# The low-rank mixing of a recurrent layer: stacked rounded operands for full fp32 products, and a new order of the pieces

## The chip, the cores and the metric

One core of one Trainium2 chip runs the kernel as a single program. The metric is device time in microseconds.
## The reference

Two layers work on 16 sequences of 1024 tokens with 256 features. Each has an attention-like part and an experts part, and adds their gated product. The change touches the recurrent part of the first layer alone. Cut to what matters:

```
delta  = shifted - h                       # h: normalised input, shifted by a token
x_lerp = h + delta * x_proj_mu
x0 = tanh(x_lerp @ xl_w1.T) @ xl_w2.T + xl_b2          # rank 32, then 5*32
x1 = tanh(x0).reshape(B, T, 5, 32)
x2 = einsum('btnr,hnr->btnh', x1, x_out_w)             # five mixes of width 256
mus = x2 + x_bias
r = (h + delta*mus[0]) @ r_w.T;  w = tanh((h + delta*mus[1]) @ w_w1.T) @ w_w2.T + w_b
k, v, g likewise from mus[2], mus[3], mus[4]
wd = exp(-exp(w))
# per step t:  o_t = r_t S + (r_t * bonus * k_t) v_t ;  S = S * wd_t + k_t v_t
# then o is normalised per head, scaled, gated by silu(g), and multiplied by o_w
```

All of it is fp32, and the result has to keep about that accuracy.

## The kernel before

Four stages follow each other: routing with the layer norm (to 282 us), the recurrence (282 to 1880), the experts of layer 0 (to 3480), and layer 1. The recurrence works on 32 groups of 512 tokens (4 sequences by 128 tokens, `GN` columns), features on partitions. The groups run in passes of four (`Fori` over j, four values of q).

Inside a group the recurrence over 128 tokens is done by seven *levels*: at level lv pairs of blocks of 2^lv tokens are joined. For each level TensorE makes 16 small products of K2 and R2 (L1408), VectorE multiplies K, R and the decay by decays (L1131 to L1135) and, at levels 0 to 4, copies the new products under a mask into A2 (L1144); ScalarE does that copy at levels 5 and 6 (L1263). Level lv + 1 needs both.

The projections of the *next* group are cut into *pieces* (0 to 9), and the output work of the previous group into *chunks*. `sequence` (L847) writes out by hand for every engine in which of nine slots s each of them comes: level s, then chunk, then piece in most slots. In slots 0 and 1 the own group's last pieces stand (values and gates). The pieces:

- piece 0: LOW, two products of `w1` with lerp, tanh on ScalarE into `low` (32 rows);
- piece 1: X0 and X0T, `w2` by `low`, tanh into `x1` (128 rows, four of the mixes) and `x1t` (32 rows, the fifth). `low`, `w2`, `xo` and `xot` are padded with zeros to 128 rows;
- pieces 2, 3, 4, 6, 7: two of the ten mixing products each (`mixes`, L1336), `xo` by `x1`, indices `MIX`. VectorE makes tmp = (product + bias) * delta (L1105), GpSimd adds h into `mix` (L1018);
- piece 3 ends with DLOW (first decay product), piece 4 with DEXP and KEY, piece 5 is REC, piece 7 begins with OWN, piece 8 is VAL, piece 9 GATES.

All these products land in two PSUM banks in turn (`bank`, L844): a product with index n may start only when the one with index n - 2 has been read (`room`, `emptied`). A product of a mix needs both halves of that mix from GpSimd (`have_mix`). `begin` makes lerp of group f + 2 on VectorE at the end of slot 8 (L1089); `ahead` makes its delta on GpSimd behind slot 7 (L1004). VectorE also does one round of the router's top-k search in each group (slots 5, 6 and 7).

Of the kernel before, what the change touches and what calls it, by code (L numbers as in the profile page):

```python
# [676 lines left out]
def recurrence_phase(nc, ctx, ps, ps_heads, xnT_d, s0_d, acc_d, left_d, ident, score, idxT, gateT, idxL, gateL, w):  # L677

    with ExitStack() as mem:
# [10 lines left out]
        w1 = sb("a_w1", [P, KD, RANK])  # L690
        w2 = sb("a_w2", [P, NMU * RANK])
        b2 = sb("a_b2", [P, 1])
        b2t = sb("a_b2t", [RANK, 1])
        xo = sb("a_xo", [P, NMU - 1, D])
        xot = sb("a_xot", [P, D])
# [17 lines left out]
        low = sb("a_low", [P, GN])  # L713
        x1 = sb("a_x1", [P, GN])
        x1t = sb("a_x1t", [P, GN])
# [55 lines left out]
        th_sb = sem("a_th_sb")  # L771
        rkb = sem("a_rkb")
# [37 lines left out]
        LOADS = 21  # L810
        PADDED = 7
# [9 lines left out]
        USES = 22  # L821
        BY_ACT = [LOW, X0, X0T, DLOW, DEXP, KEY, REC, OWN, VAL, VAL + 1]
        BY_DVE = MIX + [GATES, GATES + 1]
        AT = {2: (0, 1), 3: (2, 3), 4: (4, 5), 6: (6, 7), 7: (8, 9)}
# [19 lines left out]
        def bank(n):  # L844
            return ps[6 + n % 2]

        def sequence(eng, ahead, begin, piece, level, chunk, extra=None):  # L847

            def group(j, q, first, left):
# [11 lines left out]
                def piece_at(s):  # L861
                    if s < LATE:
                        piece(g, q, FRONT + s, first)
                    elif left:
                        piece(g + 1, f1[1], s - LATE if s < CHUNK else s - LATE + 1, False)

                for s in range(SLOTS):
                    if s < LEVELS:
                        level(g, r, s, first)
                    if left and s == CHUNK:  # L870
                        piece(g + 1, f1[1], CHUNK - LATE, False)
                    if extra and s == CHUNK:
                        extra(g, s)
                    if s < LATE or s == SLOTS - 1:
                        piece_at(s)
                        chunk_at(s)
                    else:
                        chunk_at(s)
                        piece_at(s)
                        if extra and s < CHUNK:  # L880
                            extra(g, s)
# [7 lines left out]
            for s in range(FRONT):  # L889
                piece(0, 0, s, True)  # L890
# [15 lines left out]
        def _(sp):  # L906
            loads = [(mu[:], w["L0_attn_x_proj_mu"]), (w1[:], w["L0_attn_xl_w1"]),
                     (b2[:], w["L0_attn_xl_b2"][0:P]), (b2t[:], w["L0_attn_xl_b2"][P:P + RANK]),
                     (xb[:], w["L0_attn_x_bias"]),
# [4 lines left out]
            for dst, src in loads:  # L914
                sp.dma_start(dst, src).then_inc(w_in, 16)
            padded = [(w2[0:RANK, :], w["L0_attn_xl_w2"]), (dw2[0:GATE, :], w["L0_attn_w_w2"]),
                      (xot[0:RANK, :], w["L0_attn_x_out_w"][P:P + RANK])]
            padded += [(xo[RANK * n:RANK * (n + 1), n, :], w["L0_attn_x_out_w"][RANK * n:RANK * (n + 1)])
                       for n in range(NMU - 1)]
            sp.wait_ge(set_up, PADDED)  # L920
            for dst, src in padded:
                sp.dma_start(dst, src).then_inc(w_in, 16)
            assert len(loads) + len(padded) == LOADS + 1

# [49 lines left out]
        def _(pool):  # L974
            nc.gpsimd.memset(zeros[:], 0.0).then_inc(zeroed, 1)
            for operand in (xo, w2, xot, dw2, low, x1t, dlow):
                nc.gpsimd.memset(operand[:], 0.0).then_inc(set_up, 1)
# [15 lines left out]
            pool.wait_ge(w_in, 16 * (LOADS + 1))  # L993
# [44 lines left out]
        def _(dve):  # L1038
# [32 lines left out]
            dve.wait_ge(w_in, 16 * (LOADS + 1))  # L1071
# [19 lines left out]

            def piece(f, q, s, first):
                r = q % 2
                if s == 5:
# [19 lines left out]
            def level(g, r, lv, first):  # L1114
# [5 lines left out]
                if lv == LATE:  # L1120
                    gates(g, r)
# [74 lines left out]
        def _(act):  # L1196
# [9 lines left out]
            def piece(f, q, s, first):  # L1206
                r = q % 2

                def ready(n):
                    act.wait_ge(piece_ps, USES * f + n + 1)  # L1210
                    return bank(n)
# [1017 lines left out]
```

## Time and profile before

| | us |
|---|---|
| median of 3 runs | 4614.92 |
| lowest, highest | 4613.5, 4615.97 |
| span of the profiled execution | 4612.0 |
| TensorE busy in it | 4189.6 |
| VectorE busy | 2751.5 |
| ScalarE busy | 1976.9 |
| GpSimd busy | 1694.4 |
| recurrence (one group x 32) | 282 to 1880 |

Times in rows are microseconds from the start of the profiled execution, and a duration of a row that merges several instructions reaches from the first one's start to the last one's end. Matmuls overlap: the next one starts before the end that the profile gives to the one before. A product in fp32 shows as two matmul records, one in the rounded type fp32r as one. What stands in brackets is the idle time of the engine before the row, and who ended it.

### The profile page before, as it was taken

How to read it: one execution, taken by the hardware profiler on the slowest of the kernel's cores; microseconds unless marked ns; L12 is line 12 of the kernel's file. 1: busy time of each engine (PE TensorE's matmuls, PEld its weight loads, DVE VectorE, ACT ScalarE, POOL GpSimd, SP SyncE). 2: the span in 40 equal slices, each digit the busy share in tenths (PEclk: the TensorE clock that was granted, in tenths of full speed). 3: DMA queues.
4: the chain of work that ended last, by engine and by line, in shares of the span. 5: the costliest groups of instructions: out<-in, count | busy, mean ns of one | idle time of the engine just before them, and what ended most of it. 6: DMA issues, size and time to landing. Idle time of an engine off the chain costs nothing. (4 is left out here: it accounts for less than half of the span.)

```text
span 4612.0 us, 79916 instructions
## 1 busy us (share of the span) xinstructions
PE 4189.6 (91%) x28828; PEld 3314.9 (72%) x28828; DVE 2751.5 (60%) x5151; ACT 1976.9 (43%) x3701; POOL 1694.4 (37%) x1338
## 2 busy tenths in 40 slices
PE   6759999999999999799999999999995989999985
PEld 6636555555555556698888989898995878777774
DVE  4447777777767777334343433434433688888886
ACT  2214444444444444444454444445442444444441
POOL 1123333333333333344444444444432233333333
PEclk9999999999999999899999999999997999999998
DMA  6611011011011010223223232323224334444433
GB/s 205 214 44 38 29 38 34 29 38 34 29 38 34 29 38 29 81 42 64 48 56 60 41 66 43 62 47 59 42 40 92 93 98 111 105 95 111 101 61 41
DMA packets 254043, 294.80 MB, mean 64 GB/s; under 512 B 21600, under 2 KB 226656, under 8 KB 251616
## 3 DMA queue, kind: packets, MB, share of 16 engines
q0 software_dynamic: 88064, 117.74, 15.2%
q1 hardware_dynamic: 140000, 138.26, 9.3%
q10 hardware_dynamic: 25600, 33.56, 2.2%
q8 instruction: 260, 4.26, 0.4%
q14 instruction: 119, 0.97, 0.1%
HBM read 155.15 MB, written 134.35 MB: 63 GB/s over the span
## 5 line engine op out<-in xcount | busy, mean ns | idle before, releaser
L523 DVE TENSOR_TENSOR e_hTl<-e_hf,e_hTh 128x512 fp32r<-128x512 f32 x512 | 355.0, 693 | 795.4 <-ACT e_hTh L465 795.4
L1018 POOL TENSOR_TENSOR a_mix<-a_tmp,a_h 128x512 f32<-128x512 f32 x320 | 393.9, 1251 | 808.4 <-DVE a_tmp L1105 651.9
L384 POOL DMA_INDIRECT acc_d<-e_y,e_sids x256 | 402.0, 1570 | 715.6 <-DVE e_y L539 670.8
L464 ACT ACTIVATE e_hf<-ps_heads,e_b 128x512 f32<-128x512 f32 x512 | 355.3, 694 | 697.8 <-PE ps_heads L611 690.6
L611 PE MATMUL ps<-e_w2h,e_hTh 128*128 128x256 f32 x2048 | 580.1, 283 | 0.0
L611 PE MATMUL ps<-e_w2h,e_hTl 128*128 128x256 f32 x2048 | 576.5, 281 | 0.0
L611 PE MATMUL ps<-e_w2l,e_hTh 128*128 128x256 f32 x2048 | 571.3, 279 | 0.0
L611 PE MATMUL ps_heads<-e_xTh,e_w1h 128*128 128x512 f32 x1024 | 419.4, 410 | 26.8 <-issue 22.8
L611 PE MATMUL ps_heads<-e_xTh,e_w1l 128*128 128x512 f32 x1024 | 407.6, 398 | 0.0
L611 PE MATMUL ps_heads<-e_xTl,e_w1h 128*128 128x512 f32 x1024 | 407.2, 398 | 0.4 <-issue 0.3
L611 PEld LDWEIGHTS ps<-e_w2h,e_hTh 128*128 128x128 f32 x2048 | 385.0, 188 | 19.8
L611 PEld LDWEIGHTS ps<-e_w2h,e_hTl 128*128 128x128 f32 x2048 | 385.0, 188 | 17.8
L611 PEld LDWEIGHTS ps<-e_w2l,e_hTh 128*128 128x128 f32 x2048 | 386.7, 189 | 0.0
L1408 PEld LDWEIGHTS ps_heads<-a_R,a_K 32*128 32x128 f32 x7168 | 227.0, 188 | 205.9 <-issue 204.2
L465 ACT ACTIVATE e_hTh<-ps_heads,e_b 128x512 fp32r<-128x512 f32 x512 | 351.3, 686 | 0.0
L1105 DVE SCALAR_TENSOR_TENSOR a_tmp<-ps,a_xb,a_delta 128x512 f32<-128x512 f32 x320 | 239.3, 750 | 174.9 <-PE ps L1317 160.8
L361 POOL DMA_INDIRECT e_x<-xn_d,e_gids x256 | 269.8, 1054 | 190.2 <-PE ps_heads L595 112.4
L1408 PE MATMUL ps_heads<-a_R,a_K 32*128 32x64 f32 x7168 | 256.8, 278 | 62.9 <-DVE a_A L1144 34.2
L1144 DVE COPY_PREDICATED a_A<-a_mask,ps_heads 128x1024 f32<-128x1024 uint32 x160 | 274.4, 1715 | 0.0
L1317 PE MATMUL ps<-a_x,a_xo 128*128 128x512 f32 x512 | 246.6, 604 | 0.7 <-ACT a_R L1231 0.7
L611 PEld LDWEIGHTS ps_heads<-e_xTh,e_w1h 128*128 128x128 f32 x1024 | 195.8, 191 | 66.9 <-issue 28.5
L611 PEld LDWEIGHTS ps_heads<-e_xTl,e_w1h 128*128 128x128 f32 x1024 | 195.3, 191 | 47.4
(294 smaller groups left out, 9458.6 us busy)
## 6 DMA issues: line engine op xcount, KB each, us to landing
r_x<-in_L_attn_hidden_states SPq DMA_DIRECT2D x32, 512.0 KB, 4.6
xn_d<-r_xn ACTq DMA_DIRECT2D x32, 512.0 KB, 3.1
xnT_d<-r_xT ACTq DMA_DIRECT2D x32, 512.0 KB, 3.6
acc_d<-a_zeros POOLq DMA_DIRECT2D x32, 512.0 KB, 3.0
s_d<-a_s SPq DMA_DIRECT2D x32, 512.0 KB, 2.8
e_w<-in_L_ffn_w SPq DMA_DIRECT2D x16, 1024.0 KB, 4.8
f_a<-acc_d SPq DMA_DIRECT2D x32, 512.0 KB, 3.8
f_x<-s_d SPq DMA_DIRECT2D x32, 512.0 KB, 5.2
```

Of the source, the lines that this page charges most:

```text
L361: pool.indirect_dma_start(xg[r][:, t, :], None, xn_d, bass.IndirectOffsetOnAxis(ap=gids[:, GT * q + t:GT * q + t + 1], axis=0)).then_inc(x ...
L384: pool.indirect_dma_start(acc_d, bass.IndirectOffsetOnAxis(ap=sids[:, GT * q + t:GT * q + t + 1], axis=0), ys[r][:, t, :], None, compute_o ...
L464: nc.scalar.activation(hf[m % 2][:], ps[2 + m % 2][:], ACT.Gelu, bias=b1s[:, m:m + 1])
L465: nc.scalar.activation(hT[q % 2][0][:, m, :], ps[2 + m % 2][:], ACT.Gelu, bias=b1s[:, m:m + 1]).then_inc(hi_sb, 1)
L523: nc.vector.tensor_tensor(hT[q % 2][1][:, m, :], hf[m % 2][:], hT[q % 2][0][:, m, :].bitcast(F32), ALU.subtract).then_inc(h_sb, 1)
L611: last = nc.tensor.matmul(out, lhsT, rhs, start=(first and n == 0), stop=(end and n == len(pairs) - 1))
L1018: nc.gpsimd.tensor_tensor(mix[n][:, m, :].rearrange("p (c t) -> p c t", c=GT), tmp[i % 2][:].rearrange("p (c t) -> p c t", c=GT), h[q % 2] ...
L1105: stt(out=tmp[i % 2][:], in0=bank(MIX[i])[:], scalar=xb[:, n, m:m + 1], in1=delta[r][:, m].rearrange("p c t -> p (c t)"), op0=ALU.add, op1 ...
L1144: nc.vector.copy_predicated(a4, m4.unsqueeze(1).to_broadcast([P, NH * GT, nb, half]), pairs_ps(half)).then_inc(A_sb, 1)
L1317: done = nc.tensor.matmul(to, lhsT, rhs, start=(k == 0), stop=(k == len(pairs) - 1))
L1408: done = nc.tensor.matmul(ps_heads[:, hd, c * P:c * P + P // 2].rearrange("p (n t) -> p n t", t=half), K2[r][rows, tok], R2[r][rows, tok]. ...
```

## The change

`low` and the five `x1` tiles become rounded (fp32r) operands of 128 rows: four blocks of 32 rows that hold, from the top, high, high, low, low parts of the same 32 values (the high part is the value rounded, the low part what the rounding left). The weights `w2` and `xo` hold high, low, high, low in the same rows. One rounded pass over 128 rows so adds up all four partial products, where a full fp32 product over 32 meaningful rows stood. To this end

- the host lays `w1`, `w2`, `b2` and `x_out_w` out fourfold, and `xl_w2`'s product is made once for each of the five mixes (X[0] to X[4]) instead of X0 and X0T;
- ScalarE makes the tanh into `whole[k % 2]`, 128 rows, and a rounding copy into the operand (`stack`); VectorE subtracts on rows 64 to 127 (`remainder`). That is done six times in each group (LOW and five X);
- before the first group ScalarE rounds `w2` and `xo`, and VectorE subtracts on two blocks of 32 rows of each (four instructions); GpSimd's fills with zeros shrink from seven to two, the 22 loads of weights become 17;
- there are 13 pieces, and `sequence` places them by tables, some of them between the level and the chunk of a slot, or ahead of the level. DEXP now comes ahead of level 6, the mixing products stand around DLOW, KEY and OWN instead of in pairs, and X[4] with REC comes ahead of the chunk in slot 7;
- 25 bank uses in a group instead of 22; being odd, they make the bank depend on q too.

```diff
-        LATE = 2
-        FRONT = SLOTS - LATE + 1
-        MIX = [3, 4, 5, 6, 8, 9, 13, 14, 16, 17]
-        LOW, X0, X0T, DLOW, DEXP, KEY, REC, OWN, VAL, GATES = 0, 1, 2, 7, 10, 11, 12, 15, 18, 20
-        AT = {2: (0, 1), 3: (2, 3), 4: (4, 5), 6: (6, 7), 7: (8, 9)}
+        PIECES = 13
+        AHEAD_OF_LEVEL = {6: 6, 7: 8}
+        AHEAD_OF_CHUNK = {0: 11, 1: 12, 4: 2, 5: 4, 8: 10}
+        BEHIND_CHUNK = {2: 0, 3: 1, 4: 3, 5: 5, 6: 7, 7: 9}
+        OWN_PIECES = (11, 12)
+        MIX = [4, 5, 7, 9, 11, 13, 16, 17, 18, 20]
+        X = [1, 2, 3, 6, 14]
+        LOW, DLOW, DEXP, KEY, REC, OWN, VAL, GATES = 0, 8, 10, 12, 15, 19, 21, 23
+        AT = {3: (0, 1), 5: (2, 3), 7: (4, 5), 9: (6, 7), 10: (8, 9)}
+        X_AT = {1: (0, 1), 2: (2,), 4: (3,), 8: (4,)}
...
                 for s in range(SLOTS):
+                    piece_at(AHEAD_OF_LEVEL.get(s))
                     if s < LEVELS:
                         level(g, r, s, first)
-                    if left and s == CHUNK:
-                        piece(g + 1, f1[1], CHUNK - LATE, False)
                     if extra and s == CHUNK:
                         extra(g, s)
+                    piece_at(AHEAD_OF_CHUNK.get(s))
+                    chunk_at(s)
+                    piece_at(BEHIND_CHUNK.get(s))
...
(VectorE)
+            for part, raw in ((xo, xor), (w2, w2r)):
+                for top in (RANK, 3 * RANK):
+                    nc.vector.tensor_tensor(part[top:top + RANK], raw[top:top + RANK],
+                                            part[top:top + RANK].bitcast(F32), ALU.subtract).then_inc(w_split, 1)
...
+            def remainder(f, k, part):
+                dve.wait_ge(high_sb, STACKS * f + k + 1)
+                nc.vector.tensor_tensor(part[P // 2:P, :], whole[k % 2][P // 2:P, :], part[P // 2:P, :].bitcast(F32),
+                                        ALU.subtract).then_inc(stacked, 1)
...
+                if s == 0:
+                    remainder(f, 0, low)
+                for k in X_AT.get(s, ()):
+                    remainder(f, 1 + k, x1[k])
...
(ScalarE)
+                def stack(k, n, part, **bias):
+                    to = ready(n)
+                    if not first or k >= 2:
+                        act.wait_ge(stacked, STACKS * f + k - 1)
+                    nc.scalar.activation(whole[k % 2][:], to[:], ACT.Tanh, **bias).then_inc(act_out, 1)
+                    emptied(act, f, n)
+                    nc.scalar.copy(part[:], whole[k % 2][:]).then_inc(high_sb, 1)
...
(TensorE)
+                    pe.wait_ge(stacked, STACKS * f + 2 + k)
+                    product(to[:], [(xo[:, order[k], m * P:(m + 1) * P], x1[k][:])]).then_inc(piece_ps, 1)
...
+                if s == 5:
+                    mixes(2)
+                    have_mix(0)
+                    whole_product(DLOW, GATE, [(dw1[:, k, :], mix[1][:, k, :]) for k in range(KD)])
+                    mixes(3)
+                if s == 6:
+                    emptied(pe, f, DLOW)
+                    whole_product(DEXP, P, [(dw2[:], dlow[:])])
+                if s == 7:
+                    mixes(4)
+                    have_mix(1)
+                    whole_product(KEY, P, [(kw[:, k, :], mix[2][:, k, :]) for k in range(KD)])
+                    mixes(5)
+                if s == 8:
                     have_mix(2)
+                    whole_product(REC, P, [(rw[:, k, :], mix[0][:, k, :]) for k in range(KD)])
+                if s == 10:
+                    mixes(8)
                     to = room(OWN)
...
+                    mixes(9)
```

## Rows read from the trace of the kernel before

**Rows 1.** Busy time by stretches; columns: us, busy us of each engine (instructions), clock, DMA.
```profile
800.00:1200.00 400.00, 379.37 (x3229) 235.46 (x3228) 293.22 (x445) 175.49 (x381) 141.66 (x105) 0.98 0.10 35
```

**Rows 2.** Timeline, GpSimd: start us, us, engine, line, operation, operands, count [idle before].
```profile
841.42 1.88 POOL L1004 TENSOR_TENSOR a_delta<-a_h 128x1024 f32<-128x1024 f32 x1
...
867.57 2.50 POOL L1018 TENSOR_TENSOR a_mix<-a_tmp,a_h 128x512 f32<-128x512 f32 x2 [13.24 <-DVE a_tmp L1105]
...
887.00 2.30 POOL L1018 TENSOR_TENSOR a_mix<-a_tmp,a_h 128x512 f32<-128x512 f32 x2 [6.57 <-DVE a_tmp L1105]
...
889.28 1.88 POOL L1004 TENSOR_TENSOR a_delta<-a_h 128x1024 f32<-128x1024 f32 x1
...
891.13 2.95 POOL L1018 TENSOR_TENSOR a_mix<-a_tmp,a_h 128x512 f32<-128x512 f32 x2
```

**Rows 3.** Timeline, TensorE, one group and the start of the next loop pass.
```profile
841.91 0.65 PE L1434 MATMUL ps<-a_V,a_KT 128*32 128x64 f32 x32
...
845.29 1.12 PE L1408 MATMUL ps_heads<-a_R,a_K 32*128 32x64 f32 x32
...
846.34 3.72 PE L1317 MATMUL ps<-a_vw,a_mix 128*128 128x256 f32 x16
...
856.60 1.90 PE L1317 MATMUL ps<-a_lerp,a_w 128*32 128x512 f32 x4
...
859.13 1.12 PE L1408 MATMUL ps_heads<-a_R,a_K 32*128 32x64 f32 x32 [0.62 <-DVE a_A L1144]
...
865.48 1.88 PE L1317 MATMUL ps<-a_x,a_xo 128*128 128x512 f32 x4
...
872.13 1.93 PE L1317 MATMUL ps<-a_mix,a_dw 128*64 128x512 f32 x4
...
880.13 1.88 PE L1317 MATMUL ps<-a_mix,a_rw 128*128 128x512 f32 x4
...
884.88 1.94 PE L1317 MATMUL ps<-a_x,a_xo 128*128 128x512 f32 x4
...
886.96 1.05 PE L1364 MATMUL ps<-a_heads,a_rk 128*128 128x4 f32 x8
...
895.68 0.87 PE L1408 MATMUL ps_heads<-a_R,a_K 32*128 32x64 f32 x19 [2.47 <-issue]
...
899.55 1.12 PE L1408 MATMUL ps_heads<-a_R,a_K 32*128 32x64 f32 x13 [3.00 <-issue]
...
900.60 5.21 PE L1317 MATMUL ps<-a_vw,a_mix 128*128 128x256 f32 x16
```

**Rows 4.** Timeline, VectorE, the same group.
```profile
861.09 1.24 DVE L1144 COPY_PREDICATED a_A<-a_mask,ps_heads 128x1024 f32<-128x1024 uint32 x1
...
868.96 1.40 DVE L1133 TENSOR_TENSOR a_R<-a_R,a_decays 128x256 f32<-128x256 f32 x1
...
886.08 1.52 DVE L1105 SCALAR_TENSOR_TENSOR a_tmp<-ps,a_xb,a_delta 128x512 f32<-128x512 f32 x2 [1.93 <-PE ps L1317]
...
891.89 2.74 DVE L1089 SCALAR_TENSOR_TENSOR a_lerp<-a_delta,a_mu,a_h 128x512 f32<-128x512 f32 x2
```

**Rows 5.** Timeline, TensorE, rounded products in the last stage.
```profile
3603.01 0.39 PE L2058 MATMUL ps_heads<-f_xTh,f_w1h 128*128 128x512 f32 x1
3603.24 0.39 PE L2058 MATMUL ps_heads<-f_xTh,f_w1l 128*128 128x512 f32 x1
```

**Rows 6.** Timeline, ScalarE, the same group.
```profile
861.79 0.69 ACT L1216 ACTIVATE a_x<-ps,a_b 128x512 f32<-128x512 f32 x1
```

**Rows 7.** Groups by line, experts stage; busy us, mean ns of one, idle before.
```profile
L441 ACT CAST e_w2h<-e_w 128x512 fp32r<-128x512 f32 x32 | 21.0, 656 | 0.0
...
L523 DVE TENSOR_TENSOR e_hTl<-e_hf,e_hTh 128x512 fp32r<-128x512 f32 x512 | 355.0, 693 | 795.4 <-ACT e_hTh L465 795.4
```

**Rows 8.** Timeline, TensorE, transposes behind two waits in the last stage.
```profile
3669.96 1.09 PE L2051 MATMUL ps_heads<-ident,f_xn 128*128 128x128 f32 x8 [2.81 <-ACT f_xn L1958]
...
3702.20 1.65 PE L2051 MATMUL ps_heads<-ident,f_xn 128*128 128x128 f32 x8 [2.85 <-ACT f_xn L1958]
```

More of the change, by code:

```diff
@@ L712, in recurrence_phase @@
         lerp = sb("a_lerp", [P, KD, GN])
-        low = sb("a_low", [P, GN])
-        x1 = sb("a_x1", [P, GN])
-        x1t = sb("a_x1t", [P, GN])
+        whole = [sb(f"a_whole{r}", [P, GN]) for r in range(2)]
+        low = sb("a_low", [P, GN], F32R)
+        x1 = [sb(f"a_x{k}", [P, GN], F32R) for k in range(NMU)]
         tmp = [sb(f"a_tmp{r}", [P, GN]) for r in range(2)]
@@ L809, in recurrence_phase @@
         NMM = NMU * KD
-        LOADS = 21
-        PADDED = 7
+        LOADS = 17
+        PADDED = 2
         SET = PADDED + 8
@@ L888, in sequence @@
             begin(0, 0, True)
-            for s in range(FRONT):
-                piece(0, 0, s, True)
+            for s in range(PIECES):
+                if s not in OWN_PIECES:
+                    piece(0, 0, s, True)
             ahead(1, 0, 1)
@@ L975, in _ @@
             nc.gpsimd.memset(zeros[:], 0.0).then_inc(zeroed, 1)
-            for operand in (xo, w2, xot, dw2, low, x1t, dlow):
+            for operand in (dw2, dlow):
                 nc.gpsimd.memset(operand[:], 0.0).then_inc(set_up, 1)
@@ L1346, in piece, with whole_product @@
+                    product(to[:], [(xo[:, order[k], m * P:(m + 1) * P], x1[k][:])]).then_inc(piece_ps, 1)
+                def whole_product(n, rows, pairs):
+                    product(room(n)[0:rows, :], pairs).then_inc(piece_ps, 1)
                 if s == 0:
                     pe.wait_ge(lerped, 2 * f + 2)
-                    product(room(LOW)[0:RANK, :], [(w1[:, k, :], lerp[:, k, :]) for k in range(KD)]).then_inc(piece_ps, 1)
-                if s == 1:
-                    to = room(X0)
-                    emptied(pe, f, LOW)
-                    product(to[:], [(w2[:, 0:P], low[:])]).then_inc(piece_ps, 1)
-                    to = room(X0T)
-                    pe.sem_inc(spare, 1)
-                    product(to[0:RANK, :], [(w2[:, P:P + RANK], low[:])]).then_inc(piece_ps, 1)
@@ L1356, in piece @@
-                if s == 5:
-                    to = room(REC)
+                    whole_product(LOW, P, [(w1[:, k, :], lerp[:, k, :]) for k in range(KD)])
+                for k in X_AT.get(s, ()):
+                    pe.wait_ge(stacked, STACKS * f + 1)
+                    whole_product(X[k], P, [(w2[:, order[k], :], low[:])])
+                if s in (3, 9):
+                    for i in AT[s]:
+                        mixes(i)
+                if s == 5:
+                    mixes(2)
+                    have_mix(0)
+                    whole_product(DLOW, GATE, [(dw1[:, k, :], mix[1][:, k, :]) for k in range(KD)])
+                    mixes(3)
@@ L1366, in piece @@
                     done.then_inc(piece_ps, 1)
-                for i in AT.get(s, ()):
-                    mixes(i)
-                if s == 3:
-                    to = room(DLOW)
-                    have_mix(0)
-                    product(to[0:GATE, :], [(dw1[:, k, :], mix[1][:, k, :]) for k in range(KD)]).then_inc(piece_ps, 1)
-                if s == 4:
-                    to = room(DEXP)
-                    emptied(pe, f, DLOW)
-                    product(to[:], [(dw2[:], dlow[:])]).then_inc(piece_ps, 1)
-                    to = room(KEY)
-                    have_mix(1)
-                    product(to[:], [(kw[:, k, :], mix[2][:, k, :]) for k in range(KD)]).then_inc(piece_ps, 1)
-                if s == 8:
+                    mixes(9)
+                if s == 11:
                     for u in range(2):
```

133 lines of the change are left out of this document (60 added, 73 removed).

## Prediction

> **What bounds the kernel now.** I read three views in this order. First the busy time by stretches: in the recurrence TensorE is busy 379.37 of 400 us, VectorE 293.22, ScalarE 175.49, GpSimd 141.66 [rows 1]. So TensorE is the obvious bound, and the change takes work from it. A share says nothing about what takes its place, so next come the timelines of one group (batch group of 512 tokens; 32 of them in four-group loop passes). GpSimd's delta starts at 841.42 and again at 889.28: a group takes 47.86 us [rows 2]. TensorE has a gap of 0.62 us before level 3, released by VectorE's level 2, and is otherwise all but full [rows 3]. Last, the starts of a loop pass: in every fourth group level 0 comes in two pieces after gaps of 2.47 and 3.00 us that nothing in the trace releases, and the value product behind it takes 5.21 us where 3.72 is usual [rows 3]; nothing in the change touches that, and I keep its price.
>
> Two limits thus alternate inside a group. From the lerps to level 3 VectorE leads: it works without a pause through levels 0 to 2 and what stands between them, and TensorE's level 3 at 859.13 waits for it [rows 3]. From 859.13 on TensorE leads, to the operand product of MIX 6 at 884.88, whose tmp VectorE starts at 886.08 [rows 3, 4]. Then GpSimd takes over: mix at 887.00, delta at 889.28, mix again at 891.13, and the two lerps end at 894.63 between them [rows 2, 4], which starts the next round.
>
> **What the change saves on TensorE.** An fp32 product of 512 columns is two records. Four of them started at 865.48, 0.43 apart (1.88 less the last record's 0.59, by three): a product occupies 0.85 us [rows 3]. A rounded (fp32r) product is one record, and in the last stage these start 0.23 apart (3603.01, 3603.24) and end 0.39 after their start [rows 5]. The ten mixing products go from 8.5 to 2.3 us, the two X products (1.7 us) become five of 0.23 (1.15). TensorE loses 6.2 + 0.55 = 6.8 us of a group, 218 us in 32.
>
> **What it adds.** Six times a group a tile now goes through tanh, a rounding copy on ScalarE and a subtraction on VectorE, where tanh alone stood (three times). The tanh takes 0.69 [rows 6]; the copy from SBUF to fp32r 0.656, the subtraction 0.693, both from the same forms in the experts stage [rows 7]. The subtraction works on 64 partitions here; the last stage's 64-row forms cost the same, so I take 0.69 (bounds: 0.62, since neighbours overlap, and 1.8, if it must let one GpSimd instruction of 1.15 end first). VectorE gains 3.9 us of a group, to about 39 of 47.9: no bound by its sum, but it works in order. ScalarE gains 5.8 and stays half idle. So a product's way to a usable operand becomes 0.39 + 0.69 + 0.66 + 0.69 + about 0.2 of handovers, 2.6 us, and these steps are placed in front of level work on VectorE.
>
> **The new path, step by step** (clock of the profile; level 3 still starts at 859.13, since all before it is VectorE's old work).
> 1. The low tile's subtraction comes before level 3 on VectorE. LOW ends at about 858.5 [rows 3], then 0.59 + 0.66 + 0.69: 860.5, 0.2 after VectorE was to start level 3. A level on VectorE is 0.78 of products (TensorE's level 3 ended at 860.25, handed over in 0.06, the copy began at 861.09) and the 1.24 of the predicated copy [rows 3, 4]: level 3 ends 862.5 (862.3 before).
> 2. X[0] and X[1] both stand between level 3 and level 4. ScalarE is free of the gate's activations at 861.79 [rows 6]. Tanh, copy, tanh, copy, each pair 1.3: 864.5; subtraction 865.2; level 4 on VectorE ends 867.1 (865.8 before). TensorE stands idle here; its saving of 2 us is gone.
> 3. Then subtraction, gate (the same shape) and the first tmp: 0.69 less the overlap of neighbours, twice, and half of tmp's 1.52 [rows 4, 7]: 869.1. GpSimd's two mixes need 0.17 + 1.15 + 1.15, and VectorE's K product of level 5 gets in between them with about 0.3 (three products take the 0.78 above): before, with the same three, R took 1.40 and ended at 870.36, after the second mix at 870.07 [rows 2, 4]. Both mixes are there, and DLOW starts, at 872.0. Before: 872.13 [rows 3]. All that TensorE saved up to here is gone.
> 4. DLOW 1.9, its tanh 0.6, DEXP 0.85, level 6 1.05, mix 4 0.23: KEY starts at 876.7, and mix 5 comes behind KEY's 1.71, at 878.4. Its result after 0.55, tmp 0.75, 0.17, GpSimd 1.15, 0.15: REC starts at 881.2. Before: 880.13 [rows 3]. Here TensorE waits some 2.5 us with only X[4] (0.23) in it.
> 5. REC to MIX 6 is unchanged, 4.75 us (884.88 less 880.13): 885.9. Result 0.55 later: tmp 6 starts 886.5 against 886.08 [rows 3, 4].
> 6. From tmp 6 on GpSimd's queue sets the pace, as before: first mix 0.92 later, delta 2.28 after that, and 5.35 on the lerps are done [rows 2, 4]. So the group gets 0.4 us longer, not 6.8 shorter.
>
> The sum: three of four groups +0.4. In the fourth the lerps are hidden by the loop's gap, and TensorE itself counts: MIX 8 waits for tmp 6 (887.4), OWN for tmp 7 (888.1), then 0.9 for OWN (a row of 1.05, less its last end), 0.23, and 3.4 from the state product (841.91) to level 0 (845.29) [rows 3]: level 0 at 892.6 against 845.29 + 47.86 = 893.15, -0.5. Eight passes: 8 x (3 x 0.4 - 0.5) = +5.6 us. Ahead of the first group VectorE gets four splits (widths 1280 and 640, twice; 0.69 per 512 elements gives 1.7 + 0.9 each, at most 5.2), minus the fills that GpSimd no longer makes (about 2) and a somewhat faster front (1 to 3): 0 to +3, say +1. The 1.1 MB more of weights lie beside VectorE's masks and first top-k round. Profiled time 4612 + 7 = 4619; the median stands 3 above the span: 4621, 0.15% above 4614.92. What a measurement can tell here is about 0.2%.
>
> VectorE and GpSimd alternating in step 3 is what the Trainium skill says in "SBUF — State Buffer", section "SBUF: two separate sides": an instruction of VectorE with both inputs in SBUF and one of GpSimd that reads SBUF take a shared port pair in turns, whole instruction by whole instruction. By that rule, the trace agrees: R took 1.40 and ended after the mix. The new subtractions are of this kind.
>
> **The rivals.** (a) The path is shorter than I made it. In step 6 VectorE now comes to the first lerp at about 891.3, when delta ends, 0.6 earlier than before (891.89). If the lerp goes ahead of the mix there, the lerps end 0.9 earlier than the old order gives. With step 5's +0.4 that is -0.5 in three groups, and -0.5 in the fourth as in my sum: 32 x -0.5 = -16, with the 1 us ahead and the median's 3 about 4600. For it: VectorE is no longer late. Against: delta and mix are neighbours in one queue (start to start 1.85), VectorE learns of delta by a semaphore. A handover less in steps 2 to 4 gives the same size; down to 4570.
> (b) TensorE's saving comes through for a good part, if VectorE's waits for X are not in the way of the levels. All of it is 4615 - 218 = 4397; a half, 4506. Against: steps 2 to 4 each rest on an order in the code.
> (c) Slower, by the clock. Where TensorE waits in step 4, it may come back at 1.2 GHz. In the last stage one wait of 2.81 us left the transposes behind it at 1.09 us, another of 2.85 us made them 1.65 [rows 8]; after the loop's gaps the value product took 5.21 for 3.72 [rows 3], +1.5. At +1.5 in each group: 4621 + 48 = 4669. It decides from the wait before REC: 2.5 us with 0.23 of work inside is just short of those two. The Trainium skill, "TensorE: Matmul & The Clock Gate", section "HAM oscillation — how this bites in real kernels", names gaps of idleness between bursts as what lowers the clock; by that rule this is the rival that the change invites.
> (d) Slower, by more collisions of the six subtractions with GpSimd's mixes: each costs up to 1.15. One more on the path in each group: 4621 + 37 = 4658, half of that 4640.
>
> **Chances.** My sum 0.35 (its own range 4605 to 4640: 0.25 within 0.2%, 0.03 faster, 0.07 slower); (a) 0.30 (0.27 faster, 0.03 same); (b) 0.07; (c) 0.10; (d) 0.18. Faster 0.37, same 0.28, slower 0.35. Both signs are about as likely, since the sum is a difference of two long chains in which each handover is known to 0.1 us and 32 groups multiply it. The range leaves out (b) and the ends of (a), (c): 4550 to 4665.
>
> **What would show it.** In the new profile: TensorE about 6 us idle in a group; it waits for VectorE before levels 4 and 5, and for GpSimd's mixes before DLOW and before REC (2 us or more there). VectorE waits for ScalarE at the subtraction of X[1]. From DVE tmp 6 to the lerps' end 8.5 us as now; delta to delta near 48.2. Wrong if delta to delta is under 47, if TensorE stays gapless, or if the granted clock falls in the middle of groups.

## The result and the profile after

| | us |
|---|---|
| median after (4 runs) | 4788.06 (4778.39 to 4794.64) |
| median before, same chip (4 runs) | 4615.44 (4613.5 to 4621.8) |
| ratio, 95% interval | 1.0372 (1.0357 to 1.0387) |
| span of the profiled execution after | 4793.0 |

The kernel got 3.7% slower, 173 us. I had forecast 4621 with a range to 4665; this lies outside it, beyond the price of rival (c). Each engine's line in the page, and the granted clock in 40 slices:

```profile
PE 4212.8 (88%) x28540; PEld 3433.2 (72%) x28540; DVE 2890.8 (60%) x5347; ACT 2159.2 (45%) x3991; POOL 1696.3 (35%) x1333
...
PEclk9988898888889888989999999999999899999998
```

The clock line of before:

```profile
PEclk9999999999999999899999999999997999999998
```

TensorE is busy 4212.8 us where it was 4189.6, although the change took some 218 us of products from it. The clock line says why: slices 3 to 18 hold the recurrence of after, and 13 of the 16 show an 8; in the line of before, slices 3 to 16 all show a 9, and only slice 17, in which its recurrence ends, an 8. The same stretch as [rows 1], with its columns:

```profile
800.00:1200.00 400.00, 350.02 (x2827) 243.25 (x2827) 291.39 (x439) 198.52 (x413) 131.52 (x96) 0.85 0.09 30
```

And the longer stretch by which kernels are compared below, TensorE alone (us, busy us and instructions, granted clock, DMA share, GB/s), after:

```profile
400.00:1600.00 1200.00, 1049.26 (x8549) 0.86 0.09 30
```

Before, the second one read:

```profile
400.00:1600.00 1200.00, 1143.60 (x9741) 0.99 0.10 34
```

TensorE went from 95% busy at 0.99 of full speed to 87% busy at 0.86. GpSimd's delta marks the groups. Two pairs of neighbours in the timeline of after:

```profile
369.32 1.89 POOL L1007 TENSOR_TENSOR a_delta<-a_h 128x1024 f32<-128x1024 f32 x1
417.60 1.89 POOL L1007 TENSOR_TENSOR a_delta<-a_h 128x1024 f32<-128x1024 f32 x1
...
913.47 1.88 POOL L1007 TENSOR_TENSOR a_delta<-a_h 128x1024 f32<-128x1024 f32 x1
968.09 1.89 POOL L1007 TENSOR_TENSOR a_delta<-a_h 128x1024 f32<-128x1024 f32 x1
```

One group takes 48.28 us, which is what I had forecast (48.2), another 54.62. Of the 31 distances one is 46.6, one 48.3, two are 49.8, two 51.5 to 51.7, all others 54 to 58. Before, they were 47.2 to 47.9 [rows 2], but for the first two (40.7 and 45.8) and five with the loop's gap in them, 55 to 56. The recurrence, which ended at 1880.0 before, ends at 2064.3, 184 us later; the stages behind it take 2728.7 us, where they took 2732.0.

**Where the 6.3 us of a group are.** The clock of the second group around REC and the state product, read in stretches:

```profile
903.00:907.00 4.00, 3.85 (x8) 0.58 0.34 135
907.00:913.00 6.00, 4.92 (x33) 1.00 0.00 0
913.00:925.00 12.00, 11.80 (x95) 0.57 0.16 45
925.00:947.00 22.00, 18.32 (x208) 1.00 0.01 2
```

There are two falls to 1.2 GHz (half of full speed) between this REC and the next, 2 x 0.42 x 4 = 3.4 us and 2 x 0.43 x 12 = 10.3 us long. TensorE's timeline at the same place:

```profile
901.33 0.49 PE L1346 MATMUL ps<-a_low,a_w 128*128 128x512 f32 x1 [0.45 <-ACT a_K L1254]
903.15 3.35 PE L1346 MATMUL ps<-a_mix,a_rw 128*128 128x512 f32 x4 [1.32 <-POOL a_mix L1021]
...
911.15 0.49 PE L1346 MATMUL ps<-a_x,a_xo 128*128 128x512 f32 x1 [0.77 <-DVE a_tmp L1122]
911.81 1.05 PE L1404 MATMUL ps<-a_heads,a_rk 128*128 128x4 f32 x8 [0.17 <-DVE a_tmp L1122]
...
913.64 0.93 PE L1460 MATMUL ps<-a_V,a_KT 128*32 128x64 f32 x32
...
921.73 4.88 PE L1346 MATMUL ps<-a_vw,a_mix 128*128 128x256 f32 x16
926.53 1.12 PE L1434 MATMUL ps_heads<-a_R,a_K 32*128 32x64 f32 x32
```

The group of 48.28 us:

```profile
369.55 0.65 PE L1460 MATMUL ps<-a_V,a_KT 128*32 128x64 f32 x32
...
378.17 1.12 PE L1434 MATMUL ps_heads<-a_R,a_K 32*128 32x64 f32 x32 [0.47 <-DVE a_A L1161]
...
392.33 3.23 PE L1346 MATMUL ps<-a_ow,a_og 128*128 128x256 f32 x8
...
409.13 1.98 PE L1346 MATMUL ps<-a_mix,a_rw 128*128 128x512 f32 x4 [1.09 <-POOL a_mix L1021]
...
417.83 0.65 PE L1460 MATMUL ps<-a_V,a_KT 128*32 128x64 f32 x32
```

From REC to the state product it is 10.49 us (913.64 less 903.15) against 8.70; from the state product to level 1, 12.89 (926.53 less 913.64) against 8.62. Together 6.1 of the 6.3 us. REC itself takes 3.35 for 1.98, and VAL 4.88 for the 3.72 of [rows 3]. The 48.28 us group has a fall too, at 392.33 (3.23 us where 1.89 is usual), but it takes the place of TensorE's waits before level 5 and X[3] and costs nothing: DLOW starts 9.15 us behind level 4 there and 9.31 in the second group, which has no fall at that place. So I read that a fall is paid only where the chain runs through TensorE.

### The profile page after: what moved, and what is told of

The parts are those of the page before. It is cut to its first block and busy times, and to the rows that moved or that the text cites. A ratio compares the mean times of both kernels' runs of the same rounds, so it can differ in the third digit from the quotient of the medians.

```text
span 4793.0 us, 80743 instructions
## 1 busy us (share of the span) xinstructions
PE 4212.8 (88%) x28540; PEld 3433.2 (72%) x28540; DVE 2890.8 (60%) x5347; ACT 2159.2 (45%) x3991; POOL 1696.3 (35%) x1333
## 5 line engine op out<-in xcount | busy, mean ns | idle before, releaser
L1434 PEld LDWEIGHTS ps_heads<-a_R,a_K 32*128 32x128 f32 x7168 | 251.4, 207 | 200.0 <-issue 196.3
L1434 PE MATMUL ps_heads<-a_R,a_K 32*128 32x64 f32 x7168 | 281.1, 298 | 85.4 <-DVE a_A L1161 84.1
L2025 ACT CAST f_hTh<-ps 128x512 fp32r<-128x512 f32 x160 | 93.9, 587 | 306.6 <-DVE ps L1845 306.6
L611 PEld LDWEIGHTS ps_heads<-e_xTl,e_w1h 128*128 128x128 f32 x1024 | 195.4, 191 | 47.5
```

The source lines that it names most:

```text
L611: last = nc.tensor.matmul(out, lhsT, rhs, start=(first and n == 0), stop=(end and n == len(pairs) - 1))
L1434: done = nc.tensor.matmul(ps_heads[:, hd, c * P:c * P + P // 2].rearrange("p (n t) -> p n t", t=half), K2[r][rows, tok], R2[r][rows, tok]. ...
L2025: nc.scalar.copy(hT[0][:, m, :], ps[4 + m % 2][:]).then_inc(hh_sb, 1)
```

## The experiments

My theory (A) after the result: the waits that the change opens in TensorE's queue lower its clock, twice in a group, and that is the whole loss but for a small rest. The rivals: (B) the longer chain of tanh, copy, subtraction, tmp and mix, or collisions on it, makes the groups longer, and the clock only follows; (C) the REC wait alone does it. "Filler" below is a rounded 256-column product whose result nobody reads, written to free columns of a PSUM bank; 6 of them take 0.87 us and 10 take 1.35, so one costs 0.12 while the clock is up.

All ratios are to the kernel before, measured beside each kernel. Group lengths are distances of GpSimd's deltas. "At half clock" is twice the missing share of clock, added up in stretches of 1 us over the recurrence, and beside it the number of falls. The last column is where the recurrence ends in the profiled execution (the last output product on TensorE), since the stages behind it do not take the same in all of them.

| kernel | median us | ratio (95%) | groups, us | at half clock, falls | recurrence ends |
|---|---|---|---|---|---|
| before | 4615 | 1 | 47.2 to 47.9, five of 55 to 56 | 58 us, 8 | 1880.0 |
| after | 4788.1 | 1.0372 (1.0357 to 1.0387) | six of 46.6 to 51.7; 54.2 to 57.7 | 481, 73 | 2064.3 |
| e1_fill | 4650.8 | 1.0087 (1.0069 to 1.0105) | 48.3 to 50.2, one of 46.9 | 149, 31 | 1900.3 |
| e2_fp32 | 4725.7 | 1.0244 (1.0227 to 1.0262) | 51.5 to 52.1, five of 53 to 55 | 28, 6 | 1995.4 |
| e3_rec_behind | 4730.6 | 1.0253 (1.0202 to 1.0305) | 48.8 and 53.6 in turn | 387, 53 | 1977.8 |
| e4_lean | 4800.2 | 1.0399 (1.0381 to 1.0416) | 54.6 | 666, 66 | 2067.7 |
| e7_old_rounded | 4573.2 | 0.9912 (0.9895 to 0.9928) | 45.0 to 45.3; 48.5 to 50.3 | 243, 31 | 1830.3 |
| e5_fill_all | 4635.9 | 1.0040 (1.0026 to 1.0054) | 48.8, fourth 50 to 53.5 | 43, 8 | 1902.0 |
| e10_fill_rec | 4756.3 | 1.0316 (1.0301 to 1.0331) | 48.7; 53 to 56 | 358, 49 | 2002.4 |
| e6_lean_fill | 4620.3 | 1.0013 (1.0001 to 1.0025) | 48.0, seven of 49 to 54 | 77, 11 | 1886.8 |
| e8_lean_trim | 4647.6 | 1.0068 (1.0053 to 1.0083) | 47.1; 51 to 56 | 165, 21 | 1907.7 |
| e9_rec_last | 4602.4 | 0.9977 (0.9968 to 0.9986) | 47.6, fourth 50 to 51 | 43, 8 | 1864.7 |

### e1_fill: work that nobody needs in the last four waits

```diff
+                def filler(times, key=True):
...
+                    for _ in range(times):
+                        nc.tensor.matmul(ps[4][:, HALF:2 * HALF], xo[:, 0, 0:P], xo[:, 1, 0:HALF], start=True, stop=True)
...
+                    if k == 4:
+                        filler(6, False)
...
+                    filler(10, False)
                     whole_product(REC, P, [(rw[:, k, :], mix[0][:, k, :]) for k in range(KD)])
...
+                    filler(6)
                     mixes(8)
+                    filler(2)
                     to = room(OWN)
...
+                    filler(3)
                     mixes(9)
```

> The changed kernel, and on TensorE's queue rounded products of 256 columns that nothing reads (into columns of a PSUM bank that are free there): 6 ahead of X[4], 10 ahead of REC, 6, 2 and 3 around OWN's slot, 27 in each group, all in places where TensorE waits. Theory CLOCK (TensorE comes back from its waits at 1.2 GHz; 482 us of the stage at half clock against 61 before): the clock stays up inside a group, delta to delta falls from 54.6 to about 48.2, time 4600 to 4640. Rival CHAIN (the six tanh-copy-subtract chains and the collisions make the group longer, whatever the clock): 27 more products help nothing, 4788 or more.

27 useless products in a group made the kernel 137 us faster than after. TensorE's timeline around REC:

```profile
896.16 1.35 PE L1380 MATMUL ps<-a_xo 128*128 128x256 f32 x10
897.65 1.98 PE L1346 MATMUL ps<-a_mix,a_rw 128*128 128x512 f32 x4
...
911.53 1.12 PE L1451 MATMUL ps_heads<-a_R,a_K 32*128 32x64 f32 x32 [1.65 <-issue]
```

REC takes 1.98 us again, and the two gaps of the loop's start [rows 3] have become one of 1.65. This falls to (A): under (B) a filler can at best change nothing. There are still falls (149 us), now at the output products behind levels 4 and 5, where TensorE also waits, and the median is 11 us above the range that I gave.

### e2_fp32: real work instead of fillers

```diff
-                    product(to[:], [(xo[:, order[k], m * P:(m + 1) * P], x1[k][:])]).then_inc(piece_ps, 1)
+                    product(to[:], [(xo[:, order[k], m * P:(m + 1) * P].bitcast(F32), x1[k][:].bitcast(F32))]).then_inc(piece_ps, 1)
...
-                    whole_product(X[k], P, [(w2[:, order[k], :], low[:])])
+                    whole_product(X[k], P, [(w2[:, order[k], :].bitcast(F32), low[:].bitcast(F32))])
```

> The changed kernel with its order, tiles, copies and subtractions, but the mixing and the X products are made as full fp32 products (0.85 us of TensorE each instead of 0.23). TensorE has 9 us more to do in a group, about 4 of them on the path. CLOCK: the waits get filled, the clock stays up for most of the time, 4700 to 4770, so faster than the changed kernel with more work. CHAIN: 4788 plus 4 x 32, 4900 or more.

With some 9 us more of TensorE work in each group, in the same order and with the same chains, the kernel is 62 us faster than after. The REC wait is the same (1.32), and behind it the clock does not fall (timeline of e2):

```profile
933.66 1.98 PE L1346 MATMUL ps<-a_mix,a_rw 128*128 128x512 f32 x4 [1.32 <-POOL a_mix L1021]
```

The stretch around it, clock 1.00:

```profile
930.00:936.00 6.00, 4.68 (x15) 1.00 0.22 90
```

So one wait of 1.32 us is not what does it, which speaks against (C): in after the same 1.32 stood among other waits with little work between them. Here TensorE is full ahead of it and behind it. In its groups of 51.7 us TensorE is 95% busy.

### e3_rec_behind: REC behind the first output chunk

```diff
-        PIECES = 13
+        PIECES = 14
+        REC_PIECE = 13
...
+                    if s == CHUNK:
+                        piece_at(REC_PIECE)
```

> The changed kernel with REC behind the first output chunk (K transposes and two output blocks, 3.0 us that need nothing of the mixes) instead of ahead of it, so that TensorE works where it waited for GpSimd's mixes. Without a change of the clock this takes 1.3 us out of a group: CHAIN 4788 - 42 = 4746. CLOCK: the fall at REC goes too; 4580 if the later one (around OWN) goes with it, up to 4700 if that stays.

The wait before REC goes and its fall with it, and every second group comes down to 48.8. The others stay at 53.6, with a fall of some 14 us that begins at OWN behind a wait of 0.77; in the groups of 48.8 the fall behind the same wait is 3.4 us long. The move is not clean: REC now stands late in its bank, and MIX 7 waits for ScalarE to read it, as long as REC had waited before (TensorE's timeline):

```profile
825.91 0.73 PE L1348 MATMUL ps<-a_x,a_xo 128*128 128x512 f32 x2 [1.32 <-ACT a_R L1261]
```

The median lies between the two forecasts, and the four runs spread widely (4710.3, 4710.8, 4750.5 and 4782.3; the profiled one is 4710.8). The REC wait is worth 58 to 77 of the 173 us here, not the loss: (C) falls, and e10 shows it without moving anything.

### e4_lean: e3 with shorter chains

```diff
-        MIX = [4, 5, 7, 9, 11, 13, 16, 17, 18, 20]
-        X = [1, 2, 3, 6, 14]
+        MIX = [3, 4, 6, 8, 10, 12, 16, 17, 18, 20]
+        X = [1, 2, 5, 13, 14]
...
-        X_AT = {1: (0, 1), 2: (2,), 4: (3,), 8: (4,)}
+        X_AT = {1: (0,), 2: (1,), 4: (2,), 8: (3, 4)}
```

> As e3_rec_behind, and X[1] to X[3] one slot or more later (X[1] in slot 4, X[2] in slot 5, X[3] and X[4] in slot 7), so that only one subtraction stands between the levels 3 and 4 on VectorE: 1.2 us less there. CHAIN: 4788 - 2.5 x 32 = 4708. CLOCK: 4540 to 4560 if the clock stays up, 4650 if one fall in each group is left.

The X products and their subtractions come later, only one of them between two levels. This is meant to shorten the chain that (B) blames, and the kernel came out slower than after, 4800.2, outside both forecasts. Its two falls in a group moved: one now begins at OWN, behind MIX 7's wait of 1.32 and OWN's of 0.78, one in the wait before level 4 (TensorE's timeline):

```profile
800.00 0.73 PE L1348 MATMUL ps<-a_x,a_xo 128*128 128x512 f32 x2 [1.32 <-ACT a_R L1261]
...
829.64 1.99 PE L1436 MATMUL ps_heads<-a_R,a_K 32*128 32x64 f32 x32 [1.56 <-DVE a_A L1163]
```

Its clock in the two stretches:

```profile
802.00:814.00 12.00, 12.00 (x96) 0.50 0.16 45
...
829.00:836.00 7.00, 6.36 (x43) 0.54 0.00 0
```

Level 4, 1.12 us in e1 and e5, takes 1.99 here, and VectorE waits for it. That the chain was in fact shorter is shown only by e6 and e8 below, where the clock is held.

### e7_old_rounded: the kernel before, order unchanged, one rounded pass

```diff
-                    lhsT = xo[:, n, m * P:(m + 1) * P] if n < NMU - 1 else xot[:, m * P:(m + 1) * P]
+                    lhsT = xoh[:, n, m * P:(m + 1) * P] if n < NMU - 1 else xoth[:, m * P:(m + 1) * P]
```

`low`, `x1`, `x1t` and the weights are rounded copies, and the low parts are left out; the weights are rounded by three copies before the first group. Nothing else differs from before, so inside a group there is no added copy, no subtraction and no new order.

> The kernel before with its order, tiles and chains; only the mixing and the X products are one rounded pass over the rounded values (the low parts are left out, so no copies and no subtractions). It takes TensorE's 7 us of a group away and adds nothing. CLOCK alone decides what is left of that: with the clock up a group would take 42 to 43, time 4430 to 4460; if the waits that arise lower the clock in each group as in the changed kernel, 4500 to 4650. Rival CHAIN (the added steps are what costs): 4430 to 4460, since none is added.

This isolates the saving on TensorE. Without a fall a group takes 45.0 to 45.3 where before took 47.5 to 47.9: 2.6 us come through of some 7.4 saved on TensorE (twelve products, 0.62 each). I had said 42 to 43 us a group at full clock; TensorE's waits for VectorE take the rest. But 31 falls come with the saving, and the fallen groups take 48.5 to 50.3. TensorE's waits in one group, and what stands behind them:

```profile
847.96 1.93 PE L1325 MATMUL ps<-a_mix,a_dw 128*64 128x512 f32 x4 [1.23 <-DVE a_tmp L1109]
...
852.66 1.12 PE L1325 MATMUL ps<-a_dlow,a_dw 128*128 128x512 f32 x2 [1.05 <-DVE a_tmp L1109]
...
866.01 1.17 PE L1450 MATMUL ps<-a_Sd,a_R 128*128 128x256 f32 x2
```

The product of the last row took 0.65 at 820.13, one group earlier and without a fall. The saving in an order with no new chain lowers the clock too, and the time is in the range that (A) had given, 113 us above that of (B): (A) again, and the reason is the work taken away.

### e5_fill_all: fillers in every wait of after

```diff
+                    filler(4, 5)
...
+                    filler((0, 0, 0, 5, 6)[k], 5 if s == 1 else 4)
...
+                if s == 1:
+                    filler(10, 5)
...
+                if s == 3:
+                    filler(6)
...
+                    filler(1)
...
+                    filler(1)
...
+                    filler(10)
...
+                    filler(6, 7)
...
+                    filler(2, 7)
...
+                    filler(3, 7)
```

> As e1_fill, with products that nothing reads also in the waits before the levels 3, 4 and 5, before X[3], DLOW and DEXP (59 of 256 columns in a group, each stretch shorter than its wait). Theory CLOCK: e1_fill still had one fall of the clock in each group, behind the waits before levels 3 and 4, and groups without a fall took 48.3; with those filled all groups take 48.3 and the time is 4612 - 0.6 x 31 + 15, 4590 to 4620. Rival CHAIN, in its rest: what e1_fill left of the loss (38 us over the kernel before) is the longer chains' and stays, 4650.

The edit has 54 fillers in a group, not the 59 of the text: those of e1, and more before the waits that after has at levels 3 to 5, X[3], DLOW and DEXP. The long stretch:

```profile
400.00:1600.00 1200.00, 1151.14 (x10724) 0.99 0.10 34
```

GpSimd's deltas, 48.76 apart:

```profile
805.68 1.89 POOL L1007 TENSOR_TENSOR a_delta<-a_h 128x1024 f32<-128x1024 f32 x1
854.44 1.88 POOL L1007 TENSOR_TENSOR a_delta<-a_h 128x1024 f32<-128x1024 f32 x1
```

Clock and busy share are those of before. There are 8 falls, as before, four of them behind the loop's starts and the others in the first groups and at the end, and the median is 4635.9. The order, the chains, the copies and the subtractions are all those of after: 4788.1 less 4635.9, 152 of the 173 us, are the clock, and by the end of the recurrence 162 of 184. It came out above what I expected (4590 to 4620), since some fillers run past the moment at which they should end; the groups are 48.8, where the one of after without a paid fall is 48.3. Against e1 the 27 further fillers bring the clock up but no time in the recurrence, which ends at 1902.0 for 1900.3: there, the falls that e1 had left cost next to nothing. What the 15 us between the two medians are, the profiles do not show; in them e1 is 3 us slower as a whole.

### e10_fill_rec: only the waits before X[4] and REC filled

The edit is e1's, without the last three fillers.

> The changed kernel with filling products ahead of X[4] and REC alone (16 in a group). The changed kernel's trace shows two falls in a group, one in the REC product (3.4 us at half clock), one around OWN (10.2 us). CLOCK: the first goes and the second stays, since the waits around it stay: 4740 to 4770. If the second is a consequence of the first, both go: 4650.

16 of e1's 27 fillers give 32 of its 137 us. By the recurrence alone it is 62 of 164 (it ends at 2002.4, after's at 2064.3, e1's at 1900.3): behind it 23 us are lost again, 19 of them in the experts, which are the same code and show 68 us at half clock where after shows 48; why, no run shows. Groups of 48.7 stand among groups of 53 to 56. REC takes 1.98 us in every group of the kernel but the first, so its fall is gone. The second fall, behind MIX 8, OWN and MIX 9 with waits of 0.77, 0.17 and 0.34 only, is thus the dearer one, and it comes without the first.

### e6_lean_fill, e8_lean_trim, e9_rec_last: an order that wins

e6 is e4 with 55 fillers in its waits:

```diff
+                    filler((3, 0, 5, 4, 0)[k], 5 if s == 1 else 4)
...
+                    filler(12, 5)
...
+                            filler({6: 0, 7: 9}[i], 7)
```

> e4_lean (shorter chains, yet 4800, with 666 us at half clock) with such products in its waits, 55 in a group. CLOCK: with the clock up the shorter chains show: delta to delta 46 to 47, time 4520 to 4570. Rival ORDER (what e4_lean lost was its own order of the pieces, not the clock): 4750 or more.

From e4's 4800.2 to 4620.3: 180 us off by adding work. The forecasts of 46 to 47 us a group and of 4520 to 4570 were wrong, the groups take 48.0. TensorE is now late in places: GpSimd's two mixes for DLOW end at 829.13 + 2.51 = 831.64, and DLOW starts 1 us later, behind an output product, a mix and 5 fillers. GpSimd's row:

```profile
829.13 2.51 POOL L1023 TENSOR_TENSOR a_mix<-a_tmp,a_h 128x512 f32<-128x512 f32 x2 [13.94 <-DVE a_tmp L1124]
```

TensorE's:

```profile
832.62 1.93 PE L1348 MATMUL ps<-a_mix,a_dw 128*64 128x512 f32 x4
```

e8 takes 16 of them out, so that 39 stay (not the 36 of the text; two still stand before DEXP). All those before level 5, X[2] and DLOW go:

```diff
-                    filler((3, 0, 5, 4, 0)[k], 5 if s == 1 else 4)
+                    filler((3, 0, 0, 4, 0)[k], 5 if s == 1 else 4)
...
-                    filler(5)
+                    filler(0)
```

> e6_lean_fill with 36 filling products instead of 55: none before level 5, X[2], DLOW and level 6, where e6_lean_fill's trace shows TensorE late because of them (DLOW started 832.6 where the mixes were there at 831.6). CLOCK with the longer path taken out: groups 47.2 to 47.6, time 4585 to 4605. If the clock falls again where the filling went: 4650 and more.

The groups without a fall come down to 47.1, which is 0.9 less than e6's: so much the fillers cost. But there are 10 more falls (165 us at half clock for 77), fallen groups take 51 to 56, and the median rises by 27 us, above the forecast. Not all of that is the clock: at each of the five loop starts a second gap of 2.3 to 3.4 us is back (14.6 us in all) that e6 does not have, and in the profile the experts take 17 us longer. A filler costs 0.12 us where the chain passes TensorE, a fallen group here 4 us and more, so I take the fillers for the better bargain.

e9 puts REC behind MIX 6 and 7, so that real work fills a wait, with 7 fillers ahead of it and 8 ahead of OWN:

```diff
-        MIX = [3, 4, 6, 8, 10, 12, 16, 17, 18, 20]
+        MIX = [3, 4, 6, 8, 10, 12, 15, 16, 18, 20]
...
-        LOW, DLOW, DEXP, KEY, REC, OWN, VAL, GATES = 0, 7, 9, 11, 15, 19, 21, 23
+        LOW, DLOW, DEXP, KEY, REC, OWN, VAL, GATES = 0, 7, 9, 11, 17, 19, 21, 23
```

> As e8_lean_trim, but REC stands behind the mixing products 6 and 7, not ahead of them, with its filling. In e6_lean_fill GpSimd's delta waited for tmp 7, and that for a bank held by REC; this lets delta start 2 us earlier, and the lerps then wait for tmp 9. Groups 46.5 to 47.3, time 4565 to 4600; if VectorE's end of the group (tmp 9, state, lerps) is the limit, as e8_lean_trim.

4602.4 us from 11 runs, ratio 0.9977: 0.23% below the kernel before, 2 us above my range, and the fastest of those that compute the full result. GpSimd's deltas:

```profile
845.44 1.88 POOL L1009 TENSOR_TENSOR a_delta<-a_h 128x1024 f32<-128x1024 f32 x1
893.01 1.88 POOL L1009 TENSOR_TENSOR a_delta<-a_h 128x1024 f32<-128x1024 f32 x1
942.72 1.88 POOL L1009 TENSOR_TENSOR a_delta<-a_h 128x1024 f32<-128x1024 f32 x1
```

TensorE's level 0 behind the loop's start in the same kernel:

```profile
901.15 1.12 PE L1463 MATMUL ps_heads<-a_R,a_K 32*128 32x64 f32 x32 [2.05 <-issue]
```

A usual group is 47.57, as before, and the fourth is 49.71 where before took 55.10 (889.28 to 944.38). So what this version wins, it wins at the loop's start: one gap of 2.05 where before had 2.47 and 3.00 [rows 3]. The saving of 6.8 us on TensorE has been turned into fillers, and the groups are no shorter for it.

## Why the prediction was wrong

**What limits the kernel (right).** I said that the saving would not come through, since VectorE's path to level 3 and the chain through the mixes carry the group. The 48.28 us group shows it, and e9 shows it again, with the clock up and groups of 47.6.

**Steps 1 to 6 (right).** Level 3 starts at 935.36 in the profile after, 76.23 later than the row at 859.13 on which the steps rest. Forecast times, moved by that, beside the rows:

| step | forecast | measured |
|---|---|---|
| 1. level 3 ends on VectorE | 938.7 | 938.83 |
| 2. X[1]'s subtraction ends | 941.4 | 941.32 |
| 2. level 4 ends on VectorE | 943.3 | 943.36 |
| 3. DLOW starts | 948.2 | 948.28 |
| 4. KEY starts | 952.9 | 953.40 |
| 4. REC starts | 957.4 | 957.78 |
| 5. REC to MIX 6, in the 48.28 us group | 4.75 | 4.83 |
| 6. tmp 6 to the lerps' end, same group | 8.5 | 8.46 |
| delta to delta, same group | 48.2 | 48.28 |

The rows of VectorE (timeline):

```profile
937.60 1.23 DVE L1161 COPY_PREDICATED a_A<-a_mask,ps_heads 128x1024 f32<-128x1024 uint32 x1
...
940.63 0.69 DVE L1102 TENSOR_TENSOR a_x<-a_whole,a_x 64x512 fp32r<-64x512 f32 x1 [0.49 <-ACT a_x L1239]
...
942.11 1.25 DVE L1161 COPY_PREDICATED a_A<-a_mask,ps_heads 128x1024 f32<-128x1024 uint32 x1
...
947.03 1.40 DVE L1150 TENSOR_TENSOR a_R<-a_R,a_decays 128x256 f32<-128x256 f32 x1
```

and of TensorE:

```profile
935.36 1.12 PE L1434 MATMUL ps_heads<-a_R,a_K 32*128 32x64 f32 x32 [0.66 <-DVE a_A L1161]
...
938.97 1.12 PE L1434 MATMUL ps_heads<-a_R,a_K 32*128 32x64 f32 x32 [1.32 <-DVE a_A L1161]
...
943.51 1.12 PE L1434 MATMUL ps_heads<-a_R,a_K 32*128 32x64 f32 x32 [0.80 <-DVE a_A L1161]
...
948.28 1.93 PE L1346 MATMUL ps<-a_mix,a_dw 128*64 128x512 f32 x4 [0.29 <-POOL a_mix L1021]
...
957.78 3.36 PE L1346 MATMUL ps<-a_mix,a_rw 128*128 128x512 f32 x4 [1.32 <-POOL a_mix L1021]
```

The waits that I named are all there: before levels 4 and 5 (1.32, 0.80), DLOW (0.29) and REC. The one before REC is shorter than my 2.5: 0.45 before X[4] and 1.32 behind it. R's 1.40 between the mixes is there, and the subtraction costs the 0.69 that I took. TensorE is 5.9 us idle in the 48.28 us group, I had said about 6.

**What failed: the price and the chance of the clock, in step 4 and rival (c).** In step 4 I wrote that TensorE waits some 2.5 us there, and let it restart at full speed. The fall was in rival (c) alone, at a chance of 0.10, with one fall a group at +1.5. The runs show three mistakes in it.
- The condition. I had it decide on the length of the one wait before REC, by the two waits of 2.8 us in [rows 8]. The waits behind which it falls are shorter, 0.2 to 1.4 us in the kernels after and e7, and there are several. In e2 the same 1.32 us wait has no fall behind it; in e10 a fall comes behind waits of 0.77, 0.17 and 0.34. So one wait's length does not decide. The fillers and e2 show that work in and around the waits keeps the clock up; which wait of a group tips it, they do not show. e7 shows that the falls need neither the copies nor the subtractions: the saving alone brings them.
- The count. There are two falls a group, 3.4 and 10.3 us long. I looked only at REC, since the steps named it; MIX 8, OWN and MIX 9, whose waits I had worked out myself for the fourth group, stood there to be looked at.
- The price. I took +1.5 from a value product that lies only partly in a fall. A fall costs half its length where the chain runs through TensorE: 13.7 us at half clock would be 6.9 at most, and 6.3 were lost. With it (c) would have read 4621 + 32 x 6.3 = 4823. 4788 was measured, since six of the 31 distances are shorter than 54 and the loop's gaps, which the 4621 has in it, are all but gone (below).

The Trainium skill, "TensorE: Matmul & The Clock Gate", has a section "A second HAM failure mode: psum-queue depth-cycling", on a kernel whose TensorE idles briefly between groups of products and whose clock swings for that. By that rule, the trace agrees, with waits of 0.17 to 1.32 us. I had weighed only the section on long gaps.

**The other rivals.** (a), the shorter path, did not happen. The lerp starts 2.61 behind delta as before (420.21 less 417.60; 891.89 less 889.28 in [rows 2, 4]), behind the second mix: VectorE still has the state's update to finish, until 420.2. (b) did not either; e7 puts its reach at 2.6 us a group for the rounded products with no chain in front. (d) needs a collision more in each group; the 48.28 us group, as forecast without it, excludes that.

**The front, and the loop (both mis-sized).** I gave the front +1. The splits took 3.00 + 1.67 = 4.67 us (timeline of VectorE), inside my 5.2, but the lerps of the first group start 2.85 later (285.07 for 282.22), and in the first group each X product, its copy and its subtraction stand open, with no other work beside them: TensorE waits 2.12 for the low tile's subtraction at 292.50, where it waited 0.76 for the tanh before. GpSimd's second delta in the kernel before:

```profile
312.87 1.89 POOL L1004 TENSOR_TENSOR a_delta<-a_h 128x1024 f32<-128x1024 f32 x1
```

In after:

```profile
322.69 1.89 POOL L1007 TENSOR_TENSOR a_delta<-a_h 128x1024 f32<-128x1024 f32 x1
```

In e5_fill_all:

```profile
319.62 1.90 POOL L1007 TENSOR_TENSOR a_delta<-a_h 128x1024 f32<-128x1024 f32 x1
```

It is 9.8 us late, 6.8 where the clock is held. "A somewhat faster front (1 to 3)" was a guess about the fewer loads, and no row carried it. The loop's gap I had kept at its price, and counted for eight passes. The trace of before has it at five loop starts, two pieces each time, 28.6 us in all. In after one of the five starts has a gap of 1.10 and 0.70, the others none of 0.4 or more; in e3, e4 and e10 there is none, and in e7 one of 1.60. In e1, e2, e5, e6 and e9 each of the five has one piece of 1.4 to 2.05, in e8 two pieces again. Why, no run shows.

**The account.** Of the 173 us, 152 are the clock (after less e5_fill_all, where order and chains are the same). That is what holding the clock gains net of the fillers' overrun and of the loop's gaps, which after hardly has and e5 has again (9.4 us in all), so the falls themselves cost more. The other 21 are those of e5: 6.8 for front and first group, and the rest longer groups (48.8 for 47.6, of which 0.5 are the overrun) less what the loop's shorter gap gave back against before.

**What stays open.** Why the groups of after, of e4 and the last of e3 all take 54.6 us, although their chains differ and their falls lie in other places, I did not settle. Nor why the same waits have a fall behind them in one group and none in the next: in e10 MIX 8, OWN and MIX 9 wait 0.77, 0.17 and 0.34 in both of two neighbours, and only the second falls; nor why some falls are 3.4 us long and others up to 13.7. It is not shown either how many fillers are the fewest that hold the clock; e6, e8 and e9 only bracket it, at 55, 39 and 43 a group. Fillers into columns of a bank that VectorE reads meanwhile were not tried.

## What to carry to other kernels

Before you take work from a TensorE that is nearly full (95% busy here) at full clock, ask what its clock will do: list every wait of the new order, not the longest one, and price a fall at half of its length wherever the chain passes TensorE (here 6.3 us on a group of 48.3, while the longer chain itself came to 0.4 to 0.8). If the granted clock in the profile falls in the middle of a group, put cheap products without a reader, 0.12 us each, into the waits: they took off 137 and 152 us here, and a fallen clock can be told from a longer chain by them in one run. Compare such kernels by the end of the changed stage as well as by the whole: here the same code behind it differed by up to 19 us, so that e10's 62 us in the recurrence showed as 32 in the median. And a saving on TensorE need not shorten anything where it is not the only limit: e9's gain came at the loop's start, and its groups stayed at 47.6.

## What the hardware showed that I had not expected

- TensorE 87% busy (after) ran at a granted clock of 0.86 over 1200 us, at 95% (before) at 0.99 and at 95% with the same long wait in it (e2) at 1.00. The busy share alone does not tell the clock: e4, at 91%, had 0.81. Waits of 0.2 to 1.4 us were enough for the falls of after.
- More work was faster three times: e5 over after by 152 us, e6 over e4 by 180, and e2, with 9 us a group more, over after by 62.
- An order with a shorter chain was slower (e4 over e3 by 70 us), with 666 us at half clock for 387.
- The gap at the loop's start, which nothing in the trace releases, is not fixed: 5.5 to 6.2 us in two pieces before, one of 1.4 to 2.05 in e1, e2, e5, e6 and e9, and none or next to none in after, e3, e4, e7 and e10.
